# q and k projected transposed, and the output projection moved into the attention loop, in a float32 transformer block on one Trainium2 core

## What is computed

```
mod = (silu(c) @ wmod)          # six rows of 256 for each batch
h   = layernorm(x) * (1 + ca) + sa
xn  = layernorm(h) * gamma + beta
q, k, v = heads(xn @ Wq + bq), heads(xn @ Wk + bk), heads(xn @ Wv + bv)   # 16 heads of 16
q, k = apply_rope(q), apply_rope(k)          # pairs of columns (even, odd) are rotated
probs = softmax(causal_mask(q @ k.T / 4))
x   = x + ga * (h + (probs @ v) @ Wo + bo)
```

## Time and profile before

| what | value |
|---|---|
| median of 3 runs | 3257.47 us (3256.44 to 3257.87) |
| the profiled execution | 3256.85 us, its span 3255.1 us, mean granted TensorE clock 0.952 |
| busy: TensorE | 2952.9 us (91%) |
| busy: VectorE | 2328.9 us (72%) |
| busy: ScalarE | 1713.4 us (53%) |
| busy: GpSimd | 1019.2 us (31%) |
| DMA | 403.11 MB, 124 GB/s in the mean |

### The profile page before, as it was taken

One profiled execution on the slowest core, in us unless ns is written; L12 is line 12 of the kernel. 1 busy time (PEld: TensorE's weight loads), 2 busy tenths in 40 slices (PEclk: granted clock), 3 DMA queues, 4 the chain that ended last, 5 costly groups with the idle time before them and its releaser, 6 DMA issues. The chain is left out here.

```text
span 3255.1 us, 50330 instructions
## 1 busy us (share of the span) xinstructions
PE 2952.9 (91%) x18199; PEld 1403.3 (43%) x18199; DVE 2328.9 (72%) x3444; ACT 1713.4 (53%) x3591; POOL 1019.2 (31%) x1366
## 2 busy tenths in 40 slices
PE   2888998885999999999999999999999979975997
PEld 0444444441444444444444444444444347753664
DVE  5999999995777777777777777777777425543221
ACT  1444444430677777777777777777777731111111
POOL 3888888862122111112221111112221100003232
PEclk7999999996999999999999999999999989987999
DMA  2466666657244444444444444444444246663332
GB/s 77 138 180 191 191 191 191 184 156 175 55 95 93 95 100 100 100 96 92 94 95 92 97 100 100 100 96 90 95 92 92 48 173 259 259 230 110 78 100 56
DMA packets 175373, 403.11 MB, mean 124 GB/s; under 512 B 34556, under 2 KB 87202, under 8 KB 158518
## 3 DMA queue, kind: packets, MB, share of 16 engines
q1 hardware_dynamic: 168984, 391.37, 47.1%
q0 software_dynamic: 6144, 8.52, 1.5%
HBM read 240.65 MB, written 161.31 MB: 123 GB/s over the span
## 5 line engine op out<-in xcount | busy, mean ns | idle before, releaser
L946 DVE TENSOR_REDUCE mx<-ps 128x2 f32<-128x1024 f32 (+3 forms) x1216 | 1371.2, 1166 | 396.6 <-PE ps L1034 301.3
L992 ACT ACTIVATE prob<-ps 128x512 f32<-128x512 f32 (+1 forms) x2560 | 1251.4, 561 | 539.0 <-PE ps L1052 530.0
L1027 PE MATMUL ps<-k_rows,q_rows 96*128 96x512 bf16 (+3 forms) x3072 | 909.9, 332 | 40.6 <-DMA k_rows<-k_parts 33.1
L1052 PE MATMUL ps<-q_rows,k_rows 99*128 99x512 bf16 (+3 forms) x3072 | 908.5, 329 | 14.5 <-ACT prob L992 6.0
L885 POOL TENSOR_SCALAR_AFFINE_SELECT prob<-prob 128x512 f32<-128x512 f32 x512 | 318.6, 634 | 1453.8 <-ACT prob L992 1453.8
L1071 PE MATMUL ps<-prob,v_rows 128*32 128x512 f32 (+3 forms) x6144 | 628.6, 497 | 0.0
L1052 PEld LDWEIGHTS ps<-q_rows,k_rows 99*128 99x128 bf16 x3072 | 273.3, 98 | 598.8 <-ACT prob L992 359.8
L688 PE MATMUL ps<-w_all,x_t 128*128 128x512 f32 (+1 forms) x1024 | 427.9, 543 | 0.0
L1027 PEld LDWEIGHTS ps<-k_rows,q_rows 96*128 96x128 bf16 x3072 | 290.4, 98 | 269.8 <-DVE mx L946 60.4
L1034 PE MATMUL ps<-mask_b,unit_b 128*128 128x128 bf16 (+2 forms) x1408 | 348.5, 248 | 0.0
L1071 PEld LDWEIGHTS ps<-prob,v_rows 128*32 128x32 f32 x6144 | 134.7, 108 | 245.7 <-ACT prob L992 122.8
(11 more groups left out here) (143 smaller groups left out, 2707.4 us busy)
## 6 DMA issues: line engine op xcount, KB each, us to landing
k_rows<-k_parts SPq DMA_DIRECT2D x384, 128.0 KB, 7.5
v_ones<-v_st SPq DMA_DIRECT2D x64, 512.0 KB, 9.0
v_rows<-v_ones SPq DMA_DIRECT2D x64, 512.0 KB, 9.5
att<-o_sb SPq DMA_DIRECT2D x128, 256.0 KB, 3.2
att_b<-att SPq DMA_DIRECT2D x16, 2048.0 KB, 10.9
q_parts<-stage SPq DMA_DIRECT2D x192, 128.0 KB, 2.4
k_parts<-stage SPq DMA_DIRECT2D x192, 128.0 KB, 2.4
q_rows<-q_parts SPq DMA_DIRECT2D x64, 384.0 KB, 4.6
```

Of the source, the lines that this page charges most:

```text
L946: dve.tensor_reduce(dst, src, AX.X, ALU.max).then_inc(a_free, 1)
L992: nc.scalar.activation(prob[:, (g * NPC + i) % RING, h, 0:w], src, ACT.Exp).then_inc(exp_done, 1)
L1027: ins = pe.matmul(ps[:, at, col:col + w], q[0:ROWS, g, h, i * P:(i + 1) * P], k[0:ROWS, g, h, k0:k0 + w], start=(r == 0), stop=True, skip_ ...
L1052: ins = pe.matmul(ps[:, PS_B + bank(g, n), at:at + w], k[0:AUG, g, h, j * P:(j + 1) * P], q[0:AUG, g, h, q0:q0 + w], start=True, stop=True)
```

## The change

**Phase 0** makes tables of cosine and sine with one row per rotated pair, stretched over 128 partitions (turned on TensorE), orders the columns of Wq and Wk by even and odd (16 small copies with the tables' on VectorE), and loads bq and bk as columns, in 16 small transfers.

**Phase 1** projects q and k transposed: the weights are the stationary operand, 512 rows of x the moving one. A pair n is one of q and k for 512 rows: 4 pairs a batch, each in two banks (even and odd columns). The bias matmul for q and k and the turns of q and k go. The rotation becomes four multiplications with the bias added on the way and two additions. The first tiles of a batch must all be turned and copied before its first projection. ScalarE writes xn (`second_norm`), VectorE adds the modulation's shift (`shift_h`), GpSimd no longer does. The residual is written over h1. 16 transfers of 192 KB store q and k instead of 24 of 128 KB.

**Phase 3 goes**; its work is in phase 2. SyncE fetches a batch's sums (`fetch`), VectorE inverts the sums of the exponentials (`invert`), they go to DRAM and come back spread over the 16 columns of a head, GpSimd multiplies (`normalise`), and TensorE projects 256 rows (`project`, a job) in slot TURN of a step, with no turns: the sums already have their columns on partitions. VectorE adds the residual (`add_rows`). A job runs six units behind: 58 of the 64 inside the loop. SyncE's order in a step is new: the second half's store, the maxima, what belongs to the batch before, and only then the load.

```diff
@@ phase1, vector
+            def shift_h(b, tiles):
+                for t in tiles:
+                    dve.wait_ge(h_mul, b * T + t + 1)
+                    dve.tensor_tensor(h[:, b % 2, t, :], h[:, b % 2, t, :], mods[:, b % 2, M_SA, :], ALU.add) \
+                       .then_inc(h_done, 1)
...
+            def multiply(n):
+
+                blk, which = n % NP // 2, n % 2
+                dve.wait_ge(qk_done, n + 1)
+                reuse(dve, rope_done, n)
+                at = slice(blk * W, (blk + 1) * W)
+                for m, table in ((m1, cos_t), (m2, sin_t)):
+                    for e in range(2):
+                        c = 2 * which + e
+                        ins = dve.scalar_tensor_tensor(m[:, e, :], ps[:, PS_QK + c, :], bcol[:, c:c + 1], table[:, at],
+                                                       ALU.add, ALU.mult)
+                ins.then_inc(rope_mul, 1)
+
+            def combine(n):
+
+                s = n % 2
+                dve.wait_ge(rope_mul, n + 1)
+                reuse(dve, rest_done, n - 1)
+                dve.tensor_tensor(qr[:, s, 0, :], m1[:, 0, :], m2[:, 1, :], ALU.subtract)
+                dve.tensor_tensor(qr[:, s, 1, :], m1[:, 1, :], m2[:, 0, :], ALU.add).then_inc(rope_done, 1)
+
+            def take_rest(n):
+                dve.wait_ge(hi_done, n + 1)
+                reuse(dve, lo_done, n - 1)
+                dve.tensor_tensor(rest[:, n % 2], qr[:, n % 2], parts(n, 0), ALU.subtract).then_inc(rest_done, 1)
+
+            def both(nx, fr, bk, j):
+                n = bk * NP + j // 2
+                if fr is not None and j == 0:
                     invert_x(fr)
+                if fr is not None and 1 <= j <= 4:
+                    shift_h(fr, (2 * j - 2, 2 * j - 1))
+                if fr is not None and j == 5:
+                    join_h(fr)
+                if fr is not None and j == 6:
+                    invert_h(fr)
+                if j % 2 == 0:
+                    multiply(n)
+                else:
+                    if n:
+                        take_rest(n - 1)
+                    combine(n)
+                if fr is not None and 1 <= j <= 4:
+                    take_h(fr, (2 * j - 2, 2 * j - 1))
+                if nx is not None and j in (5, 6):
+                    take_x(nx, range(4 * (j - 5), 4 * (j - 5) + 4))
+                if nx is not None and j == 7:
+                    join_x(nx)
@@ phase1, scalar
+            def both(nx, fr, bk, j):
+                n = bk * NP + j // 2
+                if j in (0, 1):
+                    for t in (4 + 2 * j, 5 + 2 * j):
+                        copy_x(bk, t)
+                if fr is not None and j < 4:
+                    first_norm(fr, (2 * j, 2 * j + 1))
+                if fr is not None and j == 5:
+                    root(fr, 1, agh, agh_done, sdh_done)
+                if fr is not None and j >= 6:
+                    second_norm(fr, range(4 * (j - 6), 4 * (j - 6) + 4))
+                if j % 2 == 0:
+                    if n:
+                        high(n - 1)
+                else:
+                    for t in (j - 1, j):
+                        copy_v(bk, t)
+                    if n:
+                        middle(n - 1)
+                if fr is not None and j >= 6:
+                    for t in (2 * j - 12, 2 * j - 11):
+                        copy_x(fr, t)
+                if nx is not None and j == 7:
+                    root(nx, 0, agx, agx_done, sdx_done)
@@ phase1, tensor
+            def project(b, n):
+
+                blk, which = n % NP // 2, n % 2
+                pe.wait_ge(xt_copied, b * T + 4 * blk + 4)
+                reuse(pe, rope_mul, n - 1)
+                for e in range(2):
+                    c = 2 * which + e
                     for k in range(KC):
+                        ins = pe.matmul(ps[:, PS_QK + c, :], w_all[:, k, c * P:(c + 1) * P], x_t[:, blk, k, :],
+                                        start=(k == 0), stop=(k == KC - 1))
+                ins.then_inc(qk_done, 1)
@@ phase2, sync
+            def fetch(b):
+
+                p, half = b % 2, b // 2
+                for c in range(2):
+                    sp.wait_ge(o_stored[c], (b + 1) * NG * DMA)
+                rows = att_d[b].rearrange("g (h n) t -> (g h) n t", h=HG)
+                reuse(sp, rec_done, b)
+                sp.dma_start(den[:, :], rows[:, DH, :].rearrange("h (x t) -> h x t", t=P)).then_inc(den_in, DMA)
+                reuse(sp, out_done, (b - 1) * PAIRS)
+                for k in range(KC):
+                    sp.dma_start(num[:, p, k, :], rows[8 * k:8 * k + 8, 0:DH, :]).then_inc(num_in[p], DMA)
+                sp.dma_start(gate[:, p], mods_d[b, M_GA, :].partition_broadcast(P)).then_inc(small_in[p], DMA)
+                sp.dma_start(ob[:, p], out_bias_d[b]).then_inc(small_in[p], DMA)
+                reuse(sp, x2_stored[p], half * DMA)
+                sp.dma_start(res[:, p], resid_d[b]).then_inc(res_in[p], DMA)
...
             def step(un, ahead):
                 b, g, u = un
                 final = isinstance(b, int) and b == LAST
                 if not (isinstance(b, int) and b == 0 and g == 0):
                     was = prior(un)
-                    if not (final and g):
-
-                        wait_apart(sp, pv_done, was[2] * NPC + NPC)
-                        load(unit(was[0], was[1] + NG))
                     store(was, 1)
+                if g == 1 and b >= 1:
+                    save_reciprocals(b - 1)
                 if not (final and g == NG - 1):
                     maxima(unit(b, g + 1))
+                if g == 0 and b >= 1:
+                    fetch(b - 1)
+                if g == 1 and b >= 1:
+                    spread_reciprocals(b - 1)
+                if u and not (final and g):
+
+                    sp.wait_ge(pv_done, was[2] * NPC + NPC)
+                    load(unit(was[0], was[1] + NG))
                 store(un, 0)
+                if g == 2 and b >= 2:
+                    store_rows(b - 2)
@@ phase2, gpsimd
+            def normalise(b):
+
+                pool.wait_ge(num_in[b % 2], (b // 2 + 1) * KC * DMA)
+                pool.wait_ge(rec_in, (b + 1) * KC * DMA)
+                for r in range(PAIRS):
+                    at = slice(r * 2 * P, (r + 1) * 2 * P)
+                    pool.tensor_tensor(num[:, b % 2, :, at], num[:, b % 2, :, at], rec_b[:, :, at], ALU.mult) \
+                        .then_inc(att_ready, 1)
...
+                    if i == 6 and un[1] == 1 and un[0] >= 1:
+                        normalise(un[0] - 1)
@@ phase2, vector
-            def whole(un, first=False):
+            def whole(un, now=None, first=False):
                 for s in range(NS):
...
+                    if s == TURN and now is not None and job_of(now[2]) is not None:
+                        add_rows(job_of(now[2]), PS_OUT)
@@ phase2, tensor
                 if s == TURN:
                     if not first and half == 0:
                         pe.wait_ge(a_free, u * NR + s - 1)
                         turn_max(prior(un))
+                    if half == 1 and j is not None:
+                        project(j, PS_OUT)
                     return
                 if half == 0 and s - 2 == TURN:
                     reuse(pe, m_left, u)
+                    if j is not None:
+                        pe.wait_ge(x2_done, j + 1)
...
+            def project(j, bank):
+
+                b, r = j // PAIRS, j % PAIRS
+                if r == 0:
+                    pe.wait_ge(wg_done, b + 1)
+                    pe.wait_ge(small_in[b % 2], (b // 2 + 1) * (2 * DMA))
+                pe.wait_ge(att_ready, j + 1)
+                for t in (2 * r, 2 * r + 1):
+                    o = ps[:, bank, (t % 2) * D:(t % 2) * D + D]
+                    pe.matmul(o, ones3[:, :], ob[:, b % 2, :], start=(t % 2 == 0), stop=False, skip_group_check=True)
+                    for k in range(KC):
+                        ins = pe.matmul(o, num[:, b % 2, k, t * P:(t + 1) * P], wg[:, b % 2, k, :], start=False,
+                                        stop=(k == KC - 1), skip_group_check=True)
+                ins.then_inc(out_done, 1)
```

792 lines of the change are left out of this document (345 added, 447 removed).

## The result

The changed kernel takes 3440.34 us (median of 4 runs, 3429.24 to 3444.51) against 3257.44 for the kernel before, run beside it: ratio 1.0557, 95% interval 1.0536 to 1.0579. It is slower by 183 us where I had forecast 103 faster. Its profiled execution took 3438.72 us, with a span of 3437.0.

The account below looks back on a forecast made before the run. VectorE was taken to bound the projection stage, TensorE the attention loop. Terms +10 + 5 - 9 - 9 + 137 + 15 - 252 = -103 us gave 3154 us (3155 on the median), range 3040 to 3240.

Parts of the forecast that it names:

- So TensorE waits about 1 us once a batch: **+15: Attention loop, first unit of a batch: load behind fetch arrives at 1476.3, needed at 1475.2; +15 us, ends 0 and +120.
- 4.1 MB a batch (247 GB/s) ... 2.7 us a MB; so fetch takes 5.9 us.: Attention loop, SyncE's queue: fetch's 2.2 MB priced by the rate of the old stage behind the loop, 5.9 us.
- In the other three units the load ends 3 to 6 us early.: Attention loop, units of a batch without fetch: the load arrives 3 to 6 us early.
- GpSimd's normalise (...) stands between selects that are far apart; its wait for the reciprocals is a rival below.: Attention loop, GpSimd: normalise fits between selects, no cost in the sum; its wait for reciprocals left to a rival.
- loads come late: Rival, attention loop: TensorE waits 8 us a batch for loads, or normalise holds selects; +105, 3260 us, no change; chance 0.13.
- half clock: Rival, projection stage: TensorE stays at 1.2 GHz, 54.8 us a batch, stage 216 us longer; 3371 us, slower; chance 0.07.
- the terms +10, +5, -9, -9: Phase 0 +10 us; first projection's wait +5; loop over 16 batches of projection -9; shorter end behind the last compute -9.
- My 1.8 us a batch for a first project at half clock: Projection stage: each batch's first project may run at 1.2 GHz, 3.6 us more; half taken, 39.5 + 1.8 = 41.3 us.
- my contended price: Projection stage, VectorE beside working GpSimd: combine 1.1 us, shift_h 0.86, take_rest 1.6; alone 0.6, 0.36, 1.14.
- free ports: Rival, projection stage: little VectorE contention with GpSimd, batch loop 36.0 us, 94 us saved instead of 9; 3070 us; chance 0.15.
- The projects: 137 predicted: Attention loop, TensorE: 58 projects of 2.36 us with no idle time to hide them, +137 us; by columns alone 1.92, +111.
- The stage that goes: Behind the attention loop: 288.2 us become a 36 us tail of the last batch (30 to 50), -252 us.

Follow-up runs that it names:

- e3: Changed kernel with the load first in SyncE's step and normalise behind the unit's last select, both edits together: 3131.3 us, ratio 0.9611 to the kernel before.
- e2: Changed kernel with only normalise moved on GpSimd, from piece 6 to behind the last select of the unit: 3426.6 us, ratio 1.0504 to the kernel before.
- e16: e12 with other numerators, read as 128 rows instead of 8 heads by 16 rows (computes wrong results): 3124.4 us, ratio 0.9592 to the kernel before.
- e6: e2 with the spread of the reciprocals put behind the load of the same unit, fetch still ahead: 3315.6 us, ratio 1.0176 to the kernel before.
- e1: Changed kernel with only the load moved, ahead of store, maxima and fetch in SyncE's step: 3285.7 us, ratio 1.0079 to the kernel before.
- e8: Kernel before with only the new phases 0 and 1, its attention loop and output projection as before: 3241.9 us, ratio 0.9950.
- e12: e2 with other rows read as 128 rows for the reciprocals (wrong results), and the residual rows behind the load: 3267.3 us, ratio 1.0035 to the kernel before.

## Why the prediction was wrong

**The step that failed** is "So TensorE waits about 1 us once a batch: **+15**", with the two sentences that lead to it. In its place stand +309 us (the changed kernel less e3); for the late loads alone, without the select's stall, it is +295 (e2 less e3). Three parts of it were wrong:

- *"4.1 MB a batch (247 GB/s) ... 2.7 us a MB; so fetch takes 5.9 us."* The price was read from transfers of 128 rows. Half of the fetch is written as 8 heads by 16 rows and moves at some 130 GB/s, 8 us a megabyte; e16 shows that, with the residual rows behind the load, this form alone makes it late. The upper end that I gave ("If fetch moved only as fast as the load (2.0 MB in 12.3 us), it would wait 8: +120") is what happened in this unit (9.26 us in the stall shown), but I did not take it, and I left out the clock behind each stall.
- *"In the other three units the load ends 3 to 6 us early."* Not in the second: the spread of the reciprocals is 1 MB of the same slow form in front of that unit's load, and it stood in no term of the loop. e6 prices it at 111 us.
- *"GpSimd's normalise (...) stands between selects that are far apart; its wait for the reciprocals is a rival below."* Far apart, but normalise waited 18 us a time, and four selects were due behind it. The rival named it and gave +105; alone it costs 154 (e1 against e3).

The rival "loads come late" was the mechanism, at 0.13. Its price was a single stall of 8 us a batch; there were two, one behind the other, and each left TensorE at the lower clock for part of the next 6 or 7 us. That is why it came to 3440 and not to this rival's 3260, and so to slower, which of the rivals only half clock had as its outcome.

The Trainium skill ("DMA: Bandwidth & Descriptors", section "Why a DMA increments its semaphore by 16 and not by 1") would have told it: a transfer runs on the largest number of engines, 16 at most, that divides the slowest dimension of both its sides. For a source of 8 by 16 rows and 128 partitions that is 8. The trace agrees: a DMA share of 0.50 to 0.53 at 125 to 131 GB/s, against 0.74 to 0.83 at 281 to 291 GB/s with 128 rows. I read the diff for bytes and issues, and not for shapes.

**Point by point, the rest held within some 15 us a term.** Phase 0: +10 predicted, 58.8 - 47.2 = +11.6. The projection phases as a whole: the terms +10, +5, -9, -9 make -3; the trace gives -14.5 and e8 -15.6. VectorE's first multiplication stands 4.9 us later in phase 1 (+5 predicted) and the end behind the last one is 7.5 us shorter (18.2 to 10.7, -9 predicted). The mis-sized term is the loop over the batches, -24 in place of -9: first multiplication to last output 666 us before, 642 after. The period of a batch was 42.2 us before and is 41.0; I had 41.9 and 41.3. My 1.8 us a batch for a first project at half clock were not there: behind a gap of some 11 us the first four turns of a batch take 1.18 us instead of 0.60, but the first project, which comes 7 us later, takes 3.7 from the second batch on (5.39 in the first). Without them my loop was 39.5, 1.5 us too short. Some of the contention that I reasoned with was there and some was not (VectorE in the projection stage of the changed kernel, mean ns behind the bar):

```profile
L464 DVE TENSOR_TENSOR h<-h,mods_b 128x256 f32<-128x256 f32 x127 | 118.1, 970 | 0.0
...
L513 DVE TENSOR_TENSOR rest<-qr,stage 128x1024 f32<-128x1024 f32 x64 | 87.3, 1364 | 1.6 <-ACT stage L600 1.6
L507 DVE TENSOR_TENSOR qr<-m 128x512 f32<-128x512 f32 x64 | 66.9, 1045 | 0.0
L508 DVE TENSOR_TENSOR qr<-m 128x512 f32<-128x512 f32 x64 | 51.5, 804 | 0.0
```

shift_h (0.97) is above my contended price of 0.86, take_rest (1.36) between the two, combine near the contended 1.1 in one half and at 0.8 in the other. The rival "free ports" is out, and so is half clock through the stage: TensorE's clock was 0.84 there and not 0.50, and the period did not reach 48. The projects: 137 predicted, 128 measured (30.4 - 28.2 = 2.2 each; 2.36 was a little too much, the 1.92 by columns too little). add_rows: no wait at slot 6, as said. The stage that goes: 288.2 us became 47.5 instead of 36, so -241 and not -252; the last batch's chain ends in a 25.5 us wait of TensorE for normalise (e3), longer than the hops I had counted. Without the failed term my sum is 3139 us; e3, the kernel without its stalls, takes 3131. That this is so near is in part luck: the front came out 12 us better and the projects 9, the stage that goes 11 us worse.

## What to carry to other kernels

Look at the outermost dimension on both sides of every new transfer before pricing it by its bytes: here 8 by 16 rows ran at 131 GB/s and 128 rows at 281 to 291. Of the 302 us between e2 (1.05 of the old time) and e16 (0.96), 124 and 143 go with the form of two transfers and 36 with the place of a third. In a queue with a fixed order, put what an engine at its limit waits for next ahead of everything that only has to be there some time later. And where two stalls stand one behind the other, undo both before judging either: alone, one edit was worth 155 us and the other 14, and the pair 309.

## What the runs showed of the hardware

- A transfer of 1 MB from a source of 8 by 16 rows keeps the DMA engines half busy (share 0.50 to 0.53, 125 to 131 GB/s) when hardly anything else is in flight. In front of a load it costs nearly the same whether each row is read 16 times or once (kernels of 3426.6 and 3405.6 us, against 3303.1 for 128 rows).
- It delays what is queued behind it by more than its bytes: 1 MB of numerators in front of a load cost 138 us over 15 batches in that form and nothing as 128 rows, though a load keeps more than half of the engines busy (0.81 in the earlier trace rows). That its parts line up behind the slow transfer on the half that carries it would explain this, and the share of one half at the end fits it (0.52 in e12, 0.97 in e16). No view here shows the engines one by one, so that it is the same half is argued and not shown.
- 128 KB as one row read 128 times cost no more than as 128 rows (3267.3 against 3269.6 us).
- After the two stalls shown, of 9.3 and 5.9 us, TensorE's mean granted clock was 0.73 and 0.66 over the next 6 us, where it is 1.00 in a unit without stalls; in the changed kernel's loop 30 such stalls cost some 70 us of slower work beside 234 us of waiting.
